# Eight GNN rounds on one core: relational batches interleaved in two parts, gathered batches prepared one step further ahead, turned rows stored by the sixth round

## What is computed

```python
# rounds 1 to 3 (SAGE), relu after the first two; third: layer norm of the sum with x
h = (segment_sum(h[src], dst) / max(count, 1)) @ Wl + bl + h @ Wr
# round 4 (GIN): msg = gelu(h[src] + edge_attr @ bond_W + bond_b) * edge_weight1
h = norm(relu(((1 + eps) * h + segment_sum(msg, dst)) @ W1 + b1) @ W2 + b2 + h)
# rounds 5 and 6 (GCN): weighted sums with self loops of weight 2, relu, layer norm, gain, shift
h = norm(relu(gcn_conv(h, edge_weight, W, b))) * g + be   # round 6: plus the residual, normed again
# rounds 7 and 8 (RGCN): one matrix per edge type, 8 types
out = segment_sum(einsum('ni,rio->rno', h, W)[etype, src], dst) + h @ loop_w + b
# round 7: relu; round 8: layer norm of the sum with round 6's result
```

## Time and profile before

| what | value |
|---|---|
| median of three runs | 6575.37 us |
| the profiled execution | 6578.35 us |
| its span in the profile | 6576.5 us |
| mean granted clock of PE | 0.876 of full speed |
| busy: PE, PE weight loads, DVE, ACT, POOL | 4754.8, 3068.4, 3341.3, 2416.9, 1892.9 us |
| DMA | 789.83 MB, mean 120 GB/s |

### The profile page before, as it was taken

How to read it: one execution, slowest core, us unless ns; L and a number is a source line. 1 busy time by engine, 2 the same in 40 slices (tenths; PEclk the granted TensorE clock), 3 DMA queues, 4 the chain that set the end, 5 groups by cost and what they waited for, 6 DMA issues and landing times. The chain is left out here.

```text
span 6576.5 us, 128477 instructions
## 1 busy us (share of the span) xinstructions
PE 4754.8 (72%) x25114; PEld 3068.4 (47%) x25115; DVE 3341.3 (51%) x10494; ACT 2416.9 (37%) x4967; POOL 1892.9 (29%) x1886
## 2 busy tenths in 40 slices
PE   5879578555577888956676666676788886777776
PEld 3445344222344555534443334342666663666663
DVE  3334233344554555546666566665344442566666
ACT  1333233133325777625554344443122222122223
POOL 4440652443204333034420432200322211322210
PEclk9989889777788999978888788888899999898899
DMA  3543465244323444334442344332233323233323
GB/s 99 160 154 134 154 193 189 94 126 128 127 94 122 142 140 143 128 100 137 137 127 91 113 130 131 123 124 92 88 103 104 98 97 113 84 97 98 100 91 100
DMA packets 429800, 789.83 MB, mean 120 GB/s; under 512 B 69304, under 2 KB 75250, under 8 KB 429716
## 3 DMA queue, kind: packets, MB, share of 16 engines
q1 hardware_dynamic: 375060, 671.58, 30.3%
q0 software_dynamic: 54656, 117.32, 7.2%
HBM read 480.10 MB, written 308.53 MB: 120 GB/s over the span
## 5 line engine op out<-in xcount | busy, mean ns | idle before, releaser
L1048 PE MATMUL p_agg<-onehot,msg 128*128 128x512 f16 (+1 forms) x2848 | 1217.2, 427 | 983.6 <-DVE onehot L1456 685.6
L642 POOL DMA_INDIRECT raw<-node_s,src_i x980 | 937.0, 956 | 2125.9 <-DVE msg L1447 952.7
L1456 DVE TENSOR_SCALAR onehot<-iota,dst_f,negbase 128x512 f16<-128x512 f16 (+1 forms) x2848 | 1063.1, 428 | 639.3 <-issue 232.8
L1050 PE MATMUL p_agg<-onehot,msg 128*128 128x512 f16 (+1 forms) x2848 | 1223.4, 430 | 0.5 <-issue 0.4
L1048 PEld LDWEIGHTS p_agg<-onehot,msg 128*128 x2848 | 292.2, 103 | 1385.4 <-issue 1258.3
L1447 DVE TENSOR_TENSOR msg<-raw,msg x140 | 163.1, 1165 | 728.5 <-ACT msg L763 660.0
L1507 DVE BATCH_NORM_STATS2 stats<-v_ring 128x6 f32 (+1 forms) x1960 | 429.1, 280 | 202.2 <-ACT v_ring L841 94.0
L642 POOL DMA_INDIRECT raw<-node_x,src_i x392 | 380.2, 970 | 430.0 <-issue 421.4
L833 ACT ACTIVATE o<-v_ring,nmr,rstd 128x128 f32 (+1 forms) x1176 | 472.2, 482 | 65.0 <-DVE nmr L1523 53.7
L803 ACT ACTIVATE u<-p_agg,sage_bias 128x512 f32<-128x512 f32 x196 | 133.8, 683 | 795.3 <-PE p_agg L1081 434.7
L1434 DVE SCALAR_TENSOR_TENSOR hid<-type_in,p_wide 128x512 f32<-128x512 f32 x448 | 253.2, 615 | 333.3 <-PE p_wide L1028 205.4
(11 more groups left out here) (258 smaller groups left out, 7953.6 us busy)
## 6 DMA issues: line engine op xcount, KB each, us to landing
node_s<-o SPq DMA_DIRECT2D x392, 256.0 KB
feature<-u SPq DMA_DIRECT2D x294, 256.0 KB
h_in<-feature SPq DMA_DIRECT2D x294, 256.0 KB
node_x<-o SPq DMA_DIRECT2D x294, 256.0 KB
res_in<-node_x SPq DMA_DIRECT2D x294, 256.0 KB
h_in<-node_x SPq DMA_DIRECT2D x196, 256.0 KB
h_in<-node_s SPq DMA_DIRECT2D x196, 256.0 KB
h_t<-dinv_scratch SPq DMA_DIRECT2D x196, 256.0 KB
```

The source lines that it names most:

```text
L642: nc.gpsimd.indirect_dma_start(out=raw[:, (e % RING) * BATCH + j, :], out_offset=None, in_=src_d, in_offset=bass.IndirectOffsetOnAxis(ap=s ...
L1048: nc.tensor.matmul(p_agg[:, a, :], tile_ap(msg, t, 0, D), oh, start=first, stop=True, skip_group_check=True)
L1050: return nc.tensor.matmul(p_agg[:, a, :], tile_ap(msg, t, D, 2 * D), oh, start=False, stop=True, skip_group_check=True)
L1456: return V.tensor_scalar(tile_ap(onehot, slot), iota[:, :], dst_f[:, bass.ds(t, 1)], negbase[:, bass.ds(it * 2 + a, 1)], ALU.subtract, ALU ...
```

## The change

Relational rounds: `turn_edges` and `products` replace the body of PE's `batch`. PE transposes part 0 of batch e + 1 between the products of part 0 and part 1 of batch e, and part 1 after them. DVE makes the masks of part 1, the low half of part 0, the masks of the next batch's part 0, and the low half of part 1. Part 1's products go to `p_tr`.

```diff
-        related = (p_edge[:, :], p_wide[:, 0, :])
+        related = (p_edge[:, :], p_tr[:, :])
 # PE, batch(e)
+                    for part in range(2):
+                        wait_apart(pe, q.lo_done, e * 2 + (part - 1))
+                        products(e, part)
+                        turn_edges(e + 1, part)
 # DVE, batch(e)
+                        masks(e, 1)
+                        low_part(e, 0)
+                        masks(e + 1, 0)
+                        low_part(e, 1)
```

```diff
-    return {... (RGCN, 1): 0, ...
+    return {... (RGCN, 1): 1, ...
+                def turn_rows(it, a):
...
+                    wait(pe, q.normed2, it + 1)
+                    wait(pe, q.turn_copied, it * 2 + a)
+                    for b in range(4):
+                        last = nc.tensor.transpose(p_tr[:, b * P:(b + 1) * P], o[:, 4 * a + b, :], ident[:, :])
+                    last.then_inc(q.turned.semaphore, 1)
 # PE, step(it) of round 6
                         layer_rows(it, 0)
+                            turn_rows(it - 3, 0)
                             for a in range(2):
                                 residual_sum(it - 2, a)
...
                             first_half(it + 1, 0, after)
+                            turn_rows(it - 3, 1)
                         layer_rows(it, 1)
 # ACT, step(it) of round 6
+                            rows_turned(it - 3, 0)
                         normalise_rows(it - 1)
+                            rows_turned(it - 3, 1)
                             second_normalise(it - 2)
 # SP, step(it) of round 6
+                            store_turned(it - 3)
                         store_rows(it - 2)
```

```diff
 # ACT
+                    if is_zero(it):
+                        each_batch(act, *batch_list(act, PT, 1), batch)
+                    if exists(it + 2):
+                        each_batch(act, *batch_list(act, PT, it + 2), batch)
 # DVE, step(it) of rounds 5 and 6
-                        these, (now, after) = even_list(dve, PT, it * 2 + 2)
-                        each_batch(dve, *these, batch)
-                        onehots(it + 1, 0, now)
+                    now, after, ahead = next_items(it)
+                    if now:
+                        onehots(it + 1, now)
                     scaled_sums(it, 1)
...
+                        first_onehots(it + 1, 1, after)
...
+                    batches_ahead(ahead)
```

```diff
-                    if e > 1:
+                    if e > 2:
                         hand_over(e - 1)
-                    elif e == 0:
-                        hand_over(0)
+                    elif e < 2:
+                        hand_over(e)
```

More of the change, by code:

```diff
@@ L32 @@
 MORE = 2
+AHEAD = RING - 1
 REL = 8
@@ L87, in __init__ @@
         self.rows_copied = one("rows_copied", NHALF)
-        self.turned = one("turned", NHALF, rows)
-        self.turn_copied = one("turn_copied", NHALF, rows)
+        self.turned = one("turned", NHALF, rows or two)
+        self.turn_copied = one("turn_copied", NHALF, rows or two)
         self.agg_done = one("agg", NHALF, rows and not rel)
-        self.feature_stored = pair("feature_stored", 16 * NPAIR, not last)
+        self.feature_stored = pair("feature_stored", 16 * NPAIR, not last or two)
         self.scaled_stored = pair("scaled_stored", 16 * NPAIR, gin)
@@ L282, in build_gnn @@
         two_ident = hid[:, 1, 0, 0:P]
+        turned_rows = [more_masked[:, 1 + a, :] for a in range(2)]
         dinv_row = h_t
@@ L879, in second_normalise @@
                     wait(act, q.moved2, it + 1)
+                    wait(act, q.turned, it * 2)
                     for a in range(2):
@@ new lines, in turn_edges, with products @@
+                def turn_edges(e, part):
+                    if part == 0:
+                        wait_apart(pe, q.copied, e + 1)
+                    j0, j1 = QUARTERS[part]
+                    for j in range(j0, j1):
+                        last = nc.tensor.transpose(p_wide[:, part, (j - j0) * P:(j - j0 + 1) * P],
+                                                   edge_v[:, j, :], ident[:, :])
+                    last.then_inc(q.et_done.semaphore, 1)
+                def products(e, part):
+                    j0, j1 = QUARTERS[part]
+                    for m in range(REL):
+                        wait(pe, q.masked_done, e * (2 * REL) + (part * REL + m + 1))
+                        for j in range(j1 - j0):
+                            last = nc.tensor.matmul(
+                                related[part][:, j * D:(j + 1) * D], masked[m][:, j * P:(j + 1) * P],
+                                w[:, m, :], start=m == 0 and j == 0, stop=True, skip_group_check=True)
+                        last.then_inc(q.masked_used.semaphore, 1)
@@ L1603, in gin_step @@
                 def gin_step(it):
-                    if exists(it + 1):
-                        these, (now, after) = even_list(dve, PT, it * 2 + 2)
-                        each_batch(dve, *these, batch)
-                        onehots(it + 1, 0, now)
+                    now, after, ahead = next_items(it)
+                    if now:
+                        onehots(it + 1, now)
                     add(it - 1, 1)
```

257 lines of the change are left out of this document (162 added, 95 removed).

## The result

The kernel after took 6331.26 us (median of four runs, 6312.18 to 6465.14) where the kernel before took 6571.24 beside it: a ratio of 0.962, 95% interval 0.957 to 0.967. One of the four runs, 6465.14 us, went at a lower clock and is left out of the ratio. The change saves 240 us, half of the 496 forecast. Faster was right; the time lies outside the range of 5960 to 6270. The profiled execution took 6339 us, span 6337.3.

A forecast was written before the change was run, and what follows sets the result against it. No engine was near 100%, PE busy 72%; batches cost time through PE's waits and slow clock, and an ACT-DVE loop in round 6. Savings less costs summed to 496 us: 6578 - 496 = 6082 us, range 5960 to 6270 (0.72).

The forecast's parts named there:

- (a): Rounds 1, 2, 3 and 5: POOL's multiply would run into the one-hots there too; price 230 us, time 6312; chance 0.07.
- Contention, -25: Shorter pairs against gathers of unchanged length: loads sharing the DMA engines become late next; 25 us lost, bounds 0 and 100.
- Round 7, 81 for batches: Round 7, masks and transposes during products: 2.9 us saved in each of 28 batches, 81 us, bounds 28 to 92.
- Round 8, 140: Round 8, masks and transposes during products: 5.0 us saved in each of 28 batches, 140 us, bounds 56 to 168.
- Batches ahead, 90: Round 6, batches made a step ahead: DVE never waits for ACT's half; 3.2 us a batch, 90 us, bounds 30 and 165.
- turning, -58: Round 6 now turns the rows: a copy in the loop (29 us) and waits (29 us) cost 58, bounds 0 and 147.
- The waits for the turn: Round 6: PE's turns wait for ACT's first copy and the second normalise; 0.6 us a pair, 29 us.
- Batches ahead elsewhere: Rounds 1, 2, 3 and 5, batches made a step ahead: 70, 42, 20 and 31 us saved.
- Start and opening: Round starts: batch 1 sooner in five rounds, 30 us; weights, constants and first one-hots moved ahead, less last turned rows, 12.
- (b): Batches were half the story: DMA contention sets rounds 1 to 3, turning eats round 6; time 6246; chance 0.04.
- (d): Rounds 7 and 8: PE waits for POOL's copy, some 10 us in each of 56 batches; 6863; chance 0.04 with kin.
- (c): Round 6 gains fully and PE runs unbroken: 5775, likelier 5930; chance 0.09 for below 5960.

## Why the forecast was half right

**The step that failed is one that is missing.** The prediction prices DVE's low half, the reading of the list and the batches, but not `more_onehots(it, 1, ...)`, which moves from the middle of a step to the start of the next. The section on the change names the move, and the sum puts it at nothing without a reason: I followed the batch that was moved and not what was split off beside it. PE waits 1.5 us at most for these one-hots in round 5's last pairs before and 5.6 after; put back, the kernel takes 0.940 for 0.962 of before, some 145 us, and 170 us of span where there is no stall (5854.9 to 5685.2). Most of those 170 us lie in rounds 3, 5 and 8 (57, 40 and 38) and in round 4 (24), which I had at 0. It fits none of the rivals: (a) has its price on the same instruction, for another reason.

**Contention, -25, was mis-sized, and by another mechanism.** Between the chips with and without the stall, the kernel before differs by 367 us of span (6576.5 to 6209.0), the kernel after by 482 (6337.3 to 5854.9): 115 us more, where 25 were priced. Taken from the chip of the plain loads the differences are 289 and 394 (6498.4 and 6248.8), 105 more. By round it grew in rounds 1, 2, 6, 7 and 8 (64 to 86, 21 to 88, 17 to 62, 58 to 98, 5 to 32) and fell in round 3 (106 to 58). The term spoke of loads that share the DMA engines; but plain loads of the same bytes took the stall away, so it was the bursts of gathers, and not the shared engines, that cost more.

**Round 7, 81 for batches.** The 3.3 us a batch counted part 1's slow products and idle time, 23.5 of 39.5 us in 12 batches, as a fault of the order. They were the gathers' stall: gone on a chip without it, in the unchanged kernel. The change could not take them away; they turned up in part 0. With the row turning, round 7 gave 79 of 144 us, and 120 where there is no stall. **Round 8, 140,** was near: 120 us in the pairs with batches, 27 of it lost in the last pairs; 158 with the one-hots back and without the stall (940.6 to 782.8).

**Round 6.** Batches ahead, 90, and turning, -58, were not to be added. Turning cost 78 with the batches ahead; batches ahead gave 36 with the turning and, from the first profile of before to the run without turning, 69 without it, moved one-hots included. The other way round, turning added 30 us to round 6 with the batches back (915.4 to 945.7) and 65 with them ahead (846.7 to 911.4). Each seems to have used the idle time of the other; the four runs lie on different chips. The waits for the turn, priced at 0.6 us a pair, cost 0.8 (39 us in 49 pairs), and the last turned rows, priced at 3, cost 13 to 14.

**Batches ahead elsewhere,** 70, 42, 20 and 31 in rounds 1, 2, 3 and 5, measured 89, 32, 32 and 39. In the stretches of these four rounds and of round 6 no wait of DVE for ACT's half is left but 2.0 us in round 2. **Start and opening:** 42, measured 48, but 20 without the stall (435.9 to 416.1), so the number was partly luck; batch 1's multiply of round 6 came 13.0 us after batch 0's, not 10.

**The rivals.** (a) had the nearest number, 6312 for 6331, and that is luck, for its mechanism did not happen: over the stretches of rounds 1, 2, 3 and 5 a one-hot takes 0.41 to 0.43 us on average, and in round 6 the collision that I had left in place went away (632 to 408 ns). The collision is real all the same: the gain began when the multiply had 1.15 us to go and took 2.24 us for 1.19 alone. The Trainium skill, SBUF — State Buffer, section "Who interferes with whom", says that DVE and GpSimd share one pair of ports and that the engine which issues later blocks entirely; by this rule, the trace agrees. (b), 6246, gave two reasons that are each half true: the gathers did hold rounds 1 to 3 back, though not by shared bandwidth, and round 6 gained nothing in sum. (d): no wait of PE for POOL's copy appears in rounds 7 and 8.

With the missing step (145) and the rest of the grown stall (115 less the 25 priced) put in, the sum is 496 - 145 - 90 = 261, for 240 measured. The parts I priced were nearly right together; without the stall and with the one-hots back they gave 524 us (6209.0 to 5685.2). Errors cancel in that: rounds 2 and 8 gave 85 and 158 for 42 and 140, the opening and round 3 only 18 and 7 for 42 and 20.

**Slips in the working.** The upper bounds together would add 521 us, so 122 is under a quarter of it, not a third. Rival (c)'s half of rounds 1 and 2 is (62 + 76)/2 = 69, not 100. In round 6, 5.92 - 1.67 - 0.93 is 3.3, not 3.2. None of them moves the forecast by more than 3 us.

## What to carry to other kernels

When a diff splits a function, follow each piece to its new place and price what waits for it there; the pairs without batches, which the change seemed not to touch, were its best test. Two costs on one idle time don't add: ask of each what is left of the slack once the other is in. And before calling idle time a matter of order, see whether it falls into a burst of gathers; here plain loads in their place showed it, and so did one more profile on another chip, without any edit.

## What was not expected of the hardware

Seven gathers in a row (0.94 us each, one every 1.24) hold up other engines on some chips and not on others: the kernel before took 6.49 to 6.58 ms in the first profile and on two chips, and 6.21 on two others. On the former PE stopped up to 1.9 us between two products of a batch, DVE waited 39.8 us, 12 times in 18 pairs of round 6, for residual sums (once until 3.5 us after the last product of the sum had ended in the records; no such entry on the latter), and single DMA issues and register instructions of SP took 0.70 us and more. PE's stops in round 8 of the kernel after, first chip:

```profile
PE p_edge L1099 <- issue: 10.2, 10, 1.9
```

SP in round 6 of the kernel after, first chip, then the same two stores and load without the stall:

```profile
3928.36 2.62 SPq L594 DMA_DIRECT2D node_x<-o  x2
3934.56 0.74 SPq L526 DMA_DIRECT2D h_in<-node_s  x1
```

```profile
3604.31 0.86 SPq L594 DMA_DIRECT2D node_x<-o  x2
3605.73 0.36 SPq L526 DMA_DIRECT2D h_in<-node_s  x1
```

From the first store to the load, 6.2 us for 1.4. Plain loads of the same size from the same queue did not do this, nor did single gathers with a landing between, on the same chip (no register or branch instruction of SP over 0.5 us in either, for 316). What tells the chips apart, and by which path a gather reaches another engine's instructions, stays open.
